# An attention-driven recurrent stage on one Trainium2 core: the query product added in PSUM to keys laid there by TensorE, and two scans in place of four vector operations

## What is computed

```
def step(h, x_t):                                   # h (8,128); enc (8,64,128)
    score = tanh(concat([h repeated over 64 positions, enc]) @ W_att) @ V_att
    attn = softmax(score)                           # over the 64 positions
    context = einsum('bs,bsh->bh', attn, enc)
    gz, gr, gh = split(concat([x_t, context]) @ Wi + b, 3)
    rz, rr, rh = split(h @ Uh, 3)
    z, r = sigmoid(gz + rz), sigmoid(gr + rr)
    hh = tanh(gh + r * rh)
    return z * h + (1 - z) * hh
```

## Time and profile before

| | us |
|---|---|
| time before, median of 3 runs (5413.26 to 5431.53) | 5423.73 |
| span of the profiled execution, first to last instruction | 5413.8 |
| PE busy, share of the span | 4614.7, 85% |
| PEld busy | 3112.5, 57% |
| DVE busy | 2884.4, 53% |
| ACT busy | 2082.3, 38% |
| POOL busy | 576.5, 11% |

### The profile page before, as it was taken

One profiled execution on the slowest core, in us unless ns is written; L12 is line 12 of the kernel. 1 busy time (PEld: TensorE's weight loads), 2 busy tenths in 40 slices (PEclk: granted clock), 3 DMA queues, 4 the chain that ended last, 5 costly groups with the idle time before them and its releaser, 6 DMA issues. The chain is left out here.

```text
span 5413.8 us, 111310 instructions
## 1 busy us (share of the span) xinstructions
PE 4614.7 (85%) x45206; PEld 3112.5 (57%) x45501; DVE 2884.4 (53%) x9511; ACT 2082.3 (38%) x4120; POOL 576.5 (11%) x1302
## 2 busy tenths in 40 slices
PE   5489999999999965889989889899778979788784
PEld 3357777777777753555555555555444756566463
DVE  6634555555555535777766677666455224433433
ACT  2223333333333312665665666566433322212221
POOL 3300111111111112111111111111000000000000
PEclk8789999999999976999999999999889989878786
DMA  0000000000000011000000000000010010000000
GB/s 26 23 18 2 2 2 2 2 2 2 2 2 2 2 61 54 4 4 6 7 6 4 4 9 4 6 1 1 1 40 1 1 44 1 1 1 1 1 1 9
DMA packets 32272, 49.22 MB, mean 9 GB/s; under 512 B 8244, under 2 KB 23638, under 8 KB 31136
## 3 DMA queue, kind: packets, MB, share of 16 engines
q1 hardware_dynamic: 28448, 38.27, 2.2%
q10 hardware_dynamic: 2304, 2.11, 0.1%
q0 software_dynamic: 1024, 1.78, 0.1%
HBM read 37.72 MB, written 4.19 MB: 8 GB/s over the span
## 5 line engine op out<-in xcount | busy, mean ns | idle before, releaser
L2299 DVE TENSOR_REDUCE l_m<-psum 128x2 bf16<-128x512 f32 x768 | 503.8, 692 | 148.8 <-PE psum L1904 146.5
L2175 ACT ACTIVATE l_probs<-psum,l_mcol 128x1024 f32<-128x1024 f32 x384 | 406.3, 1109 | 159.2 <-PE psum L1942 159.2
L1184 PE MATMUL psum<-g_gx,ident 128*128 128x128 f32 x1536 | 416.0, 389 | 18.0
L1173 PE MATMUL psum<-g_still,ident_bf 128*128 128x256 bf16 (+3 forms) x1551 | 391.5, 281 | 1.7 <-PEq L58 1.7
L1904 PE MATMUL psum<-l_kb,l_qmb 32*128 32x256 bf16 x1536 | 295.4, 273 | 56.1 <-DVE l_m L2299 52.4
L1252 ACT ACTIVATE g_th<-g_pre 128x256 f32<-128x256 f32 x512 | 191.7, 417 | 314.3 <-DVE g_pre L1285 314.3
L1184 PEld LDWEIGHTS psum<-g_gx,ident 128*128 128x128 f32 x1536 | 279.4, 195 | 12.8
L1942 PE MATMUL psum<-l_qm,l_keys 32*128 32x256 f32 x3072 | 265.1, 418 | 13.3 <-issue 13.3
L2186 ACT COPY l_heads_out<-psum 128x256 f32<-128x256 f32 (+1 forms) x292 | 130.0, 445 | 369.8 <-PE psum L1968 186.3
L1285 DVE TENSOR_TENSOR g_pre<-g_encp,psum 128x256 f32<-128x256 f32 x512 | 192.8, 418 | 132.9 <-PE psum L1202 122.4
L2299 DVE TENSOR_REDUCE l_cm<-psum 128x4 bf16<-128x256 f32 x400 | 166.0, 427 | 179.8 <-PE psum L1904 179.6
(11 more groups left out here) (567 smaller groups left out, 9761.9 us busy)
## 6 DMA issues: line engine op xcount, KB each, us to landing
s_w<-in_S_w SPq DMA_DIRECT2D x16, 256.0 KB, 5.0
f_w<-in_F_w SPq DMA_DIRECT2D x2, 2048.0 KB, 12.5
l_wf<-in_L_W SPq DMA_DIRECT2D x6, 576.0 KB, 3.8
l_w<-in_L_W SPq DMA_DIRECT2D x1, 3072.0 KB, 10.6
l_nw<-in_L_nw SPq DMA_DIRECT2D x1, 2304.0 KB, 8.0
l_wc<-in_L_W SPq DMA_DIRECT2D x6, 384.0 KB, 3.0
h_w<-in_H_W ACTq DMA_DIRECT2D x16, 129.0 KB, 3.0
h_w<-in_H_W SPq DMA_DIRECT2D x16, 129.0 KB, 3.0
```

What stands on the lines that cost most here:

```text
L1173: pe.matmul(psum[:, bank, 0:cols], cst["ident_bf"][:], still[:, 0:cols], start=True, stop=True)
L1184: pe.matmul(psum[:, bank, 0:P], cst["ident"][:], repeated(gx(gate, s)), start=True, stop=False)
L2175: act.activation(probs[:, u % 2, chunk, :].rearrange("p (g n) -> p g n", g=GROUP), psum[:, 0:GROUP, S * chunk:S * chunk + S], ACT.Exp, bia ...
L2299: dve.tensor_reduce(place, psum[:, c.bank(("max", u, g)), 0:x.tiles * x.width] .rearrange("p (t k) -> p t k", t=x.tiles), AX.X, ALU.min)\
```

## The change

It rewrites the second pass; the sizes and the number of steps stay.

- Keys and query meet in PSUM. `keys_part(i)` lays 256 key columns into a bank of its own (0 and 7) with an identity as weights; `query_part(i)` adds `wa` times the state there, each state column repeated 64 times as the moving operand. ScalarE takes the tanh straight out of PSUM. The vector additions `pre`, the two query products before, and `wa_half` are gone.
- The state is kept as pairs, `h` [128, 2, 8, 2], with the state in the second place of each pair, so its 8 columns lie 8 bytes apart.
- The candidate's bank holds pairs too: first half of U h, then the input's share plus half of U h plus the context's share (`GXC`, `uh_half`, `paired`). One `tensor_tensor_scan` with factors (0, tr) makes the candidate's input, and one with factors (0, 1-z) the new state (listings of the compiled program name both SCALAR_TENSOR_TENSOR, with 128x16). They take the place of `u`, `u2` and `part`, and of GpSimd's sum.
- The order of TensorE's list is another: the input's shares of all three gates for the next step stand ahead of its query, the reset gate's state product stands between the two halves of the scores, and the keys of the next step at two places. No `keep_busy` is left inside the steps (18 stand ahead of them, as before).
- GpSimd clears `GXC` once, and in each step halves the state and stores it.

```diff
-        GX = sb("gx", [P, 3, B, S])
+        GX, GXC = sb("gx", [P, 2, B, S]), sb("gxc", [P, B, S, 2])
...
-        h = sb("h", [P, 2, B])
-        pre, th = sb("pre", [P, 2, PAIRS, C]), sb("th", [P, 2, PAIRS, C])
+        h0, half = sb("h0", [P, B]), sb("half", [P, B])
+        h = sb("h", [P, 2, B, 2])
+        uh_half = sb("uh_half", [P, D])
+        th = sb("th", [P, 2, PAIRS, C])
...
+        reset, u = sb("reset", [P, B, 2]), sb("u", [P, B, 2])
+        decay, addend = sb("decay", [P, B, 2]), sb("addend", [P, B, 2])
...
+                pool.memset(GXC[:], 0.0).then_inc(sig["shares_cleared"], 1)
...
+                    dst = GX[:, i, 2 * p:2 * p + 2, :] if i < 2 else GXC[:, 2 * p:2 * p + 2, :, 1]
...
-                        if s == 0:
-                            pe.matmul(psum[:, 0, 0:B], wa[:, 0, :], hs, start=True, stop=True)\
-                                .then_inc(sig["query_ready"], 1)
-                        else:
-                            pe.wait_ge(sig["kept_part_ready"], s)
-                            pe.matmul(psum[:, 0, 0:P], wa_half[:], repeated(zh[:]), start=True, stop=False)
-                            pe.wait_ge(sig["new_part_ready"], s)
-                            pe.matmul(psum[:, 0, 0:B], wa[:, 0, :], part[:], start=False, stop=True)\
-                                .then_inc(sig["query_ready"], 1)
-                            keep_busy(3, 256)
-                            pe.wait_ge(sig["state_ready"], s)
-                        pe.matmul(psum[:, 7, 0:P], uh[:, 2, :], repeated(hs), start=True, stop=True)\
-                          .then_inc(sig["state_products_ready"], 1)
-                        if s >= 1:
-                            pe.wait_ge(sig["tanh_z_ready"], s)
-                        input_part(0, 4, s)
-                        if s >= 1:
-                            pe.wait_ge(sig["candidate_input_ready"], s)
-                        input_part(2, 6, s)
...
-                        pe.matmul(psum[:, 5, 0:P], uh[:, 1, :], repeated(hs), start=False, stop=False)
-                        pe.matmul(psum[:, 4, 0:P], uh[:, 0, :], repeated(hs), start=False, stop=False)
-                        keep_busy(3, 256)
...
-                        keep_busy(3, 320, 2)
...
-                        keep_busy(3, 192)
-                        pe.wait_ge(sig["context_z_taken"], s + 1)
-                        turn_part(2, 4, "gate_z_ready")
-                        keep_busy(3, 512)
-                        if s + 1 < STEPS_A_PASS:
-                            pe.wait_ge(sig["tanh_r_ready"], s + 1)
-                            input_part(1, 5, s + 1)
-                            keep_busy(3, 256)
...
-                            act.activation(th[:, i, :, :], pre[:, i, :, :], ACT.Tanh).then_inc(sig["tanh_ready"], 1)
...
-                        dve.wait_ge(sig["query_ready"], s + 1)
-                        query = psum[:, 0, 0:B].rearrange("p (b i) -> p i b", i=2)
-                        for i in range(2):
-                            dve.tensor_tensor(pre[:, i, :, :], encp[:, i, :, :],
-                                              query[:, i, :].unsqueeze(2).to_broadcast([P, PAIRS, C]), ALU.add)\
-                                .then_inc(sig["tanh_input_ready"], 1)
...
-                        dve.wait_ge(sig["tanh_r_ready"], s + 1)
-                        dve.wait_ge(sig["state_products_ready"], s + 1)
-                        dve.scalar_tensor_tensor(u[:], tr[:], 1.0, psum[:, 7, 0:B], ALU.add, ALU.mult).then_inc(sig["reset_ready"], 1)
-                        dve.wait_ge(sig["gate_h_ready"], s + 1)
-                        dve.wait_ge(sig["reset_ready"], s + 1)
-                        dve.scalar_tensor_tensor(u2[:], u[:], 0.5, psum[:, 6, 0:B], ALU.mult, ALU.add)\
-                            .then_inc(sig["candidate_input_ready"], 1)
-                        dve.wait_ge(sig["tanh_z_ready"], s + 1)
-                        if s >= 1:
-                            dve.wait_ge(sig["state_ready"], s)
-                        dve.scalar_tensor_tensor(zh[:], tz[:], 1.0, h[:, s % 2, :], ALU.add, ALU.mult)\
-                            .then_inc(sig["kept_part_ready"], 1)
-                        steps.after(dve.tensor_scalar(omz[:], tz[:], -0.5, 0.5, ALU.mult, ALU.add))
-                        dve.wait_ge(sig["candidate_ready"], s + 1)
-                        dve.tensor_tensor(part[:], omz[:], cand[:], ALU.mult).then_inc(sig["new_part_ready"], 1)
...
+            def repeated(cols, n=REPEATS):
+                return cols.unsqueeze(1).to_broadcast([P, n, B])
+            KEY_BANKS = (0, 7)
+            candidate = psum[:, 6, 0:2 * B].rearrange("p (b two) -> p b two", two=2)
...
+                def paired(cols):
+                    return cols.unsqueeze(1).to_broadcast([P, REPEATS // 2, B, 2])
+                def candidate_input(s):
+                    pe.matmul(psum[:, 6, 0:P], cst["ident"][:], paired(GXC[:, :, s, :]), start=True, stop=False)
+                def keys_part(i):
+                    pe.matmul(psum[:, KEY_BANKS[i], 0:PAIRS * C], cst["ident"][:], encp[:, i, :, :].rearrange("p b s -> p (b s)"),
+                              start=True, stop=False)
+                def query_part(i, hs):
+                    pe.matmul(psum[:, KEY_BANKS[i], 0:PAIRS * C], wa[:, 0, :],
+                              hs[:, i::2].unsqueeze(2).to_broadcast([P, PAIRS, C]), start=False, stop=True)\
+                        .then_inc(sig["tanh_input_ready"], 1)
+                def score_rows(i):
+                    for p in range(PAIRS):
+                        last = pe.matmul(psum[32 * p:32 * p + 32, 1, 0:C], vneg[:, i, :], th[:, i, p, :],
+                                         start=i == 0, stop=i == 1)
+                    return last
...
+                def turn_part(i, out, ready):
+                    pe.matmul(out, crows[:, i, :], shares[:], start=False, stop=True).then_inc(sig[ready], 1)
+                keep_busy(3, 512, 18)
+                input_part(1, 5, 0)
+                input_part(0, 4, 0)
+                candidate_input(0)
+                keys_part(0)
+                keys_part(1)
+                for s in range(S):
+                    hs = h[:, s % 2, :, 1]
+                    if s:
+                        pe.wait_ge(sig["state_ready"], s)
+                    query_part(0, hs)
+                    query_part(1, hs)
+                    pe.wait_ge(sig["tanh_ready"], 2 * s + 1)
+                    score_rows(0)
+                    pe.matmul(psum[:, 5, 0:P], uh[:, 1, :], repeated(hs), start=False, stop=False)
+                    pe.wait_ge(sig["tanh_ready"], 2 * s + 2)
+                    score_rows(1).then_inc(sig["scores_ready"], 1)
+                    if s + 1 < S:
+                        keys_part(0)
+                    pe.matmul(psum[:, 4, 0:P], uh[:, 0, :], repeated(hs), start=False, stop=False)
+                    pe.wait_ge(sig["exp_ready"], s + 1)
+                    for i in range(2):
+                        last = pe.matmul(psum[C * i:C * i + C, 2, 0:B], attn[:], pick[:, i, :], start=True, stop=True)
+                    last.then_inc(sig["attn_turned"], 1)
+                    pe.matmul(psum[:, 6, 0:P], uh_half[:], paired(hs.unsqueeze(2).to_broadcast([P, B, 2])), start=False, stop=False)
+                    pe.wait_ge(sig["attnT_ready"], s + 1)
+                    context_part(1, 3, "context_r_ready")
+                    context_part(2, 1, "context_h_ready")
+                    context_part(0, 2, "context_z_ready")
+                    pe.wait_ge(sig["shares_ready"], s + 1)
+                    pe.wait_ge(sig["context_r_taken"], s + 1)
+                    turn_part(0, psum[:, 5, 0:B], "gate_r_ready")
+                    pe.wait_ge(sig["context_h_taken"], s + 1)
+                    turn_part(1, candidate[:, :, 1], "gate_h_ready")
+                    pe.wait_ge(sig["context_z_taken"], s + 1)
+                    turn_part(2, psum[:, 4, 0:B], "gate_z_ready")
+                    if s + 1 < S:
+                        keys_part(1)
+                        pe.wait_ge(sig["tanh_r_ready"], s + 1)
+                        input_part(1, 5, s + 1)
+                        pe.wait_ge(sig["tanh_z_ready"], s + 1)
+                        input_part(0, 4, s + 1)
+                        pe.wait_ge(sig["candidate_input_ready"], s + 1)
+                        candidate_input(s + 1)
+            @block.scalar
+            def _(act):
+                for s in range(S):
+                    for i in range(2):
+                        act.wait_ge(sig["tanh_input_ready"], 2 * s + i + 1)
+                        act.activation(th[:, i, :, :], psum[:, KEY_BANKS[i], 0:PAIRS * C].rearrange("p (b s) -> p b s", s=C), ACT.Tanh)\
+                            .then_inc(sig["tanh_ready"], 1)
...
+                    act.activation(reset[:, :, 1], psum[:, 5, 0:B], ACT.Tanh, scale=0.5).then_inc(sig["tanh_r_ready"], 1)
...
```

(42 more changed lines are left out.)

128 lines of the change are left out of this document (39 added, 89 removed).

## The result

The changed kernel takes 5608.31 us (median of 4 runs, 5604.33 to 5614.43) against 5427.11 for the kernel before (4 runs, 5413.26 to 5431.53): ratio 1.0346, 95% interval 1.0321 to 1.0371. (The table before the prediction had three of those four runs of the kernel before, hence its 5423.73.) The forecast was 5600 in a range of 5510 to 5760. The profiled execution took 5604.33 us, with a span of 5602.5.

What follows compares the result with a forecast made beforehand. A chain across three engines, PE's list just fitting, bounds the 5.90 us step. 0.49+0.07+0.10+0.05 = 0.71 us a step, times 255, is 181 us; on the 5413.8 span plus 9.9, about 5605, said as 5600, range 5510 to 5760.

Steps and rivals of the forecast that it cites:

- context to query: Step's end up to the query's start on PE: +0.49 us, all from the part after the update gate's turn.
- query to end of scores: From the query's start to the scores' end: +0.07 us, the state product between the halves delaying the second.
- to the turning: From scores to the exponentials' turning: +0.10 us, as PE has keys and a state product there.
- to the context: From the turning to the context: +0.05 us, 0.65 with `uh_half` against 0.59 now.
- the tail: From the update gate's turn to the query on PE: 1.15 us becomes 1.64, +0.49.
- The credit of 0.1 for an earlier turn: Before the query: the update gate's turn starts some 0.1 us earlier, since zeros of 192 columns ahead of it go.
- State first, PE later: At the step's end: the new state is ready 0.5 to 0.6 us before PE reaches its query; VectorE's saving is idle time.
- Layout: State products 8 bytes apart and pairs cost as contiguous, 0.23 us each; rival of slow strided reads, 5650 to 5805, chance 0.12.
- a gain of 0.18: Query to scores' end: without the state product between the score halves, 1.82 us instead of 2.00.
- Scans: One scan over 16 elements replaces two dependent operations of 0.16 us; it costs 0.17 to 0.20.
- The clock: PE's clock stays 1.00 in the steps; rival: it falls without the zeros, 6300 to 6400 if always, chance 0.07.
- The price given: Steps with PE's clock always low: +3 us a step, from some 36 records of 128 columns on the path.

Runs made afterwards that it cites:

- Run 2: Changed kernel with two more dependent VectorE copies ahead of the second scan, to bring the state 0.44 us later: 5591.81 us, ratio 1.0326.
- run 1: Changed kernel with the input shares of reset and update gates laid out with a step's 8 columns side by side: 5503.11 us, ratio 1.0163.
- run 4: Changed kernel with the reset gate's state product behind both score halves, and the update gate's and candidate's input shares behind the query: 5510.68 us.
- run 3: Changed kernel with the reset gate's state product moved from between the two halves of the scores to behind them: 5607.3 us, ratio 1.0357.
- run 6: Changed kernel with the layout of run 1, the order of run 4, and the update gate's state product behind the context: 5422.23 us, ratio 1.0026.
- run 12: Run 11 with a query of 8 columns instead of 128, and zeros of 768 columns behind it for 512: 5397.17 us, ratio 0.9954.
- run 8: Changed kernel with input shares and state products over their 8 columns (16 in the pairs) once, without repeats: median 6476.52 us, ratio 1.1873.
- run 9: Kernel before without the seven matmuls of zeros in each step: 5718.84 us, ratio 1.0589.
- run 10: Kernel before with the layout of run 7 and without the seven matmuls of zeros in each step: 5725.82 us, ratio 1.0597.
- run 7: Kernel before with its three input shares laid out with a step's 8 columns side by side: 5397.3 us, ratio 0.997.
- run 11: Run 7 plus pairs, both scans and GpSimd's new part, VectorE additions kept, a 128-column query, two shares behind it: 5416.3 us, ratio 1.0015.

## Why the prediction was right, point by point

**The sum.** 0.71 us a step was forecast, 0.78 measured. With the context's start as a mark that both have (in the earlier trace rows 1512.66, less a period of 5.90: 1506.76):

| from, to | before | after | measured | forecast |
|---|---|---|---|---|
| context to query | 2.61 | 3.21 | +0.60 | +0.49 |
| query to end of scores | 2.00 | 2.06 | +0.06 | +0.07 |
| to the turning | 0.70 | 0.78 | +0.08 | +0.10 |
| to the context | 0.59 | 0.63 | +0.04 | +0.05 |

The total agreed better than the sum did. In the steps 198 us were added where 181 were forecast, yet the medians differ by just 181.2. Of the missing 17 us, 10 are the shorter rest of the profiled execution; what remains is less than executions of one kernel differ among themselves (10 and 18 us). This closeness of 5608 to 5600 is luck; what was right is the four terms, three of them within 0.02.

**The one term that was mis-sized is the tail.** It priced the keys at 0.43 as contiguous, pitch 0.22. The group L1193 behind the turns takes 0.68; less a record of 0.379 (L1197) that is a pitch of 0.30. Its weight load starts at 1504.26, only 0.03 ahead of its first matmul, where the shares behind it have theirs ahead by 0.22 (1504.59 to 1504.81). The forecast itself counted such a load for the keys behind the scores (0.32+0.22), and left it out here. That is 0.09 of the missing 0.11; it is read from the rows, and no run took it away by itself. The credit of 0.1 for an earlier turn nearly held: the turn's first record, the fifth of the six of L1216, starts 1.37 behind the context's start in the trace, where it was 1.46 (1508.22 less 1506.76). The rest is rounding.

**State first, PE later** was forecast at 0.5 to 0.6 us and is 0.75, of which the keys' weights are 0.09. Run 2 shows it: 0.41 more on the way to the state costs nothing. Runs 1 and 4 show that the list ahead of the query does count: 0.43 comes back by shortening two strided shares, 0.36 net by moving two shares behind it.

**Layout.** That the state and the pairs cost what contiguous columns do held: 273 and 281 ns against 274. The Trainium skill, "Advanced Engine Details and Errata", section SBUF Cachelines, gives 16-byte lines and asks two hits on each for full rate; the trace agrees for 8 bytes (273 ns) and for 1024 (392 ns). Steps between were not run.

**The scores.** The first half starts 1.07 behind the query as forecast, the second at 1.74 (forecast 1.75), 0.29 behind its tanh's end. That the state product is what holds it is shown by run 3 (1.81 for the end of the scores, 1.82 forecast). That this would be a gain of 0.18 was only true of that place: as long as products and keys stand ahead of the turning, the whole gain is held there, and run 6 had to move a product out of that place for 0.11.

**Scans.** 187 and 191 ns (forecast 170 to 200), tanh from PSUM 384 (380). Runs 2 and 12 show the rest: no gain and no loss from them.

**The clock** stayed at 1.00, but the rival stood nearer than a chance of 0.07 makes it look. The forecast argued that keys and query stream more columns than the zeros had; run 8 still has these, lacks only the repeats, and loses the clock. So the reason given was not the one that holds, and that this rival stayed away was partly luck. Runs 8 to 10 show that both kernels hold it by work that no result needs: zeros before, repeated columns after. The price given was +3 us a step if the clock is always low. Run 8 has +3.47, but with fewer columns, so it doesn't measure that price directly.

**What was not asked in the forecast** is whether the keys in PSUM could pay at all. Run 6 has keys and scans, run 12 the scans alone, run 7 neither. Means over 140 steps of each trace, us:

| from, to | run 6 | run 7 | run 12 |
|---|---|---|---|
| context to query | 2.63 | 2.57 | 2.52 |
| query to end of scores | 1.94 | 1.98 | 2.00 |
| to the turning | 0.78 | 0.69 | 0.69 |
| to the context | 0.64 | 0.60 | 0.64 |
| step | 5.99 | 5.84 | 5.85 |

From query to scores the keys do win something, 0.06 against run 12: the tanh starts 0.74 behind the query instead of 0.88. (Run 6's first scores come late, 1.51 behind the query where run 7 has 1.32, since PE is through with the two input shares behind the query only then; but the end of the scores is what the chain goes on from.) They lose it again elsewhere. Keys stand ahead of the turning, 0.09; and the update gate's product, moved behind the context, makes the turn of the rows 0.11 later. So no order that was run makes the keys pay. Whether another one would, and the keys without the scans, were not tried. The keys take at least 0.86 us of PE's time in each step, two matmuls of 0.43.

## What to carry to other kernels

When a vector operation is moved into a matmul on an engine that is in the chain itself, price its columns by the pitch in the trace, list what stands ahead of the first instruction on the path, and compare its end with the time at which its operand is ready: here keys and two more shares ahead of the query (0.52, 0.43 and 0.24 us) turned a shorter vector chain into idle time. Of work that needs no fresh operand, only as much belongs ahead of a waited-for instruction as fits into the wait. Before zeros or repeated columns are taken out as useless, look at the granted clock in the windows of the version without them.

## What the runs showed of the hardware that I had not expected

- The recorded busy share of PE doesn't tell which clock it gets. The granted clock is 0.50 at 100% busy (run 8), 0.68 at 95% (run 9), and 1.00 in run 11, where PE is busy 89%:

```profile
440.00:640.00 200.00, 177.38 (x2253) 132.69 (x2290) 96.44 (x436) 59.93 (x234) 12.65 (x68) 1.00 0.01 2
```

- A float32 matmul of 256 columns behind matmuls of 8 columns shows its weight load: 0.30 us between its two records (L1193) instead of 0.22 (L1197).
- A scan over 16 elements costs 187 to 191 ns, some 20 more than the 165 to 168 of an operation on 8 (L1317, L1318), though it does the work of two operations.
- Where the matmuls change from 32 to 128 weight columns, 0.15 us lie between the starts of the last record before and the first one after (1506.98+0.32-0.22 = 1507.08 to 1507.23); between records of 128 columns at full width it is 0.11. The Trainium skill, "TensorEngine Tiling (Array Packing)", section Key Properties, says that a change of tiling mode drains the engine; it gives no figure. The rows fit that, but can't show the cause.
